# Where the load of x stands in SyncE's order: before or after the two transposes of a step

## The chip, the cores and the metric

The kernel runs on all 8 cores of one Trainium2 chip. Every core runs the same program on its own eighth of the tokens, and the cores do not talk to each other. The time is the device time of the slowest core in microseconds (us). Before the change it is 530.05 us, the median of three runs (528.37 to 530.62).

## What is computed

The input x is 2 x 16384 tokens of 1024 numbers. With xn the layer norm of x (no gain, no bias), the reference returns x + s * g:

```python
B = xn @ W2 + b2;  C = xn @ W3 + b3              # 16 columns each
delta = softplus(xn @ W1 + b1)                   # 1024 columns
h = xn[..., None] * einsum('bld,bln->bldn', delta, B)
s = einsum('bln,bldn->bld', C, h)                # = xn * delta * sum(B * C)
xh = xn @ H                                      # H: Hadamard matrix / 32
scale = max(abs(xh), axis=-1) / 7
xq = clip(round(xh / scale), -8, 7) * scale      # 4-bit activations
g = silu(xq @ tern(weight).T)                    # tern: -1, 0, +1 times a scale per row
```

## The kernel before

Each core has 4096 tokens, as 32 tiles of 128 tokens. A tile passes through a software pipeline. Each of the five engines has its own instruction stream with the same loop, `for c in range(-4, nt + 4)` with nt = 32, and in step c an engine works for several tiles, each at another stage. Semaphores alone tie the streams together. A waiting instruction holds up all that stands behind it on its engine. On ACT, DVE and POOL a helper (`Ser`, line 33) records every operation, so their line in the profile is always L33 and one goes by the names of the tiles.

What happens to tile t, with the step in which it happens:

- SyncE (SP in the profile) loads x into one of ten buffers, `xbuf[t % 10]` (**xb**), in step t-5 (line 176). From tile 10 on it waits first until the output tile that used the buffer is ready (semaphore sVOUT, line 175).
- ScalarE (ACT) squares and sums the tile in step t-4 (`dumpa<-xb`, called **the square** here; it is the first operation of an ACT step and waits for the load). VectorE (DVE) sums it in the same step (`xsm<-xb`). ACT makes the normalised bf16 tile `xnb` in step t-2.
- SyncE transposes xnb into **xnT** by a DMA in step t-2 (line 183), after a wait for xnb (line 179).
- GpSimd (POOL) makes sum and difference of the halves of xnT, uT and vT, in step t-1. TensorE (PE) multiplies xnT by W2 and W3 in step t-1 (line 303), by W1 (lines 268, 269) and, through uT and vT, by the Hadamard matrix (lines 312, 314) in step t.
- ACT makes delta in step t, and in step t+1 it rounds to 4 bits: `xqm`, then **xqb**.
- SyncE transposes xqb into **xqT** in step t+1 (line 191), after a wait for xqb (line 188).
- PE multiplies xqT by the ternary weight in step t+2 (lines 289, 290). In step t+3 DVE copies the product (`o3s`) and ACT makes the sigmoid from it with three operations (`esb<-psO`, `l`, `s`); they are the last of an ACT step.
- POOL and DVE combine in step t+4: t1b (POOL), t3b (DVE), t4b and ob (POOL), and POOL issues the store of the output tile (line 238).

So SyncE, whose stream holds nothing but DMAs and waits, goes in step c through three of them: the load of tile c+5, the transpose of xnb of tile c+2, the transpose of xqb of tile c-1. The load of tile c+5 is wanted by the square at the head of ACT's step c+1. The first five tiles are loaded ahead of the loop (line 169).

Of the kernel before, what the change touches and what calls it, by code (L numbers as in the profile page):

```python
# [62 lines left out]
def build_nc(nt=NT):  # L63
    tpc = nt * 128
    nc = bass.Bass("TRN2", target_bir_lowering=False)
    x_hbm = nc.dram_tensor("x", [tpc, DM], F32, kind="ExternalInput").ap()
# [14 lines left out]
    with ExitStack() as es:  # L81
# [22 lines left out]
        xbuf = [S(f"xb{i}", [128, DM], F32) for i in range(10)]  # L104
# [32 lines left out]
        sLDa = [SEM(f"sLD{i}") for i in range(10)]  # L137
# [22 lines left out]
        @block.sync  # L160
        def _(sp):
            sp.dma_start(out=c160s[:], in_=c160_hbm[:]).then_inc(sC160, 16)
            sp.dma_start(out=nc160s[:], in_=nc160_hbm[:]).then_inc(sC160, 16)
            sp.dma_start(out=identbf[:], in_=identbf_hbm[:]).then_inc(sWS, 16)
            sp.dma_start(out=identf[:], in_=identf_hbm[:]).then_inc(sWS, 16)
            sp.dma_start(out=onesbf[:], in_=onesbf_hbm[:]).then_inc(sWS, 16)
            sp.dma_start(out=onesf[:], in_=onesf_hbm[:]).then_inc(sWS, 16)
            for t in range(min(5, nt)):
                sp.dma_start(out=xbuf[t % 10][:], in_=x_hbm[t * 128:(t + 1) * 128, :]).then_inc(sLDa[t % 10], 16)
            sp.dma_start(out=Hs[:], in_=h_hbm[:]).then_inc(sWS, 16)  # L170
            for c in range(-4, nt + 4):
                t = c + 5
                if 5 <= t < nt:
                    if t >= 10:
                        sp.wait_ge(sVOUT, t - 9)
                    sp.dma_start(out=xbuf[t % 10][:], in_=x_hbm[t * 128:(t + 1) * 128, :]).then_inc(sLDa[t % 10], 16)
                t = c + 2
                if 0 <= t < nt:
                    sp.wait_ge(sXNB, t + 1)
                    if t >= 3:  # L180
                        sp.wait_ge(sPEBC, t - 1)
                        sp.wait_ge(sUVT, t - 2)
                    sp.dma_start(out=xnT[t % 3][:].rearrange("p (c n) -> p c n", c=KC),
                                 in_=xnbf[t % 8][:].rearrange("p (c n) -> p c n", c=KC),
                                 transpose=True).then_inc(sTXNa[t % 3], 16)
                t = c - 1
                if 0 <= t < nt:
                    sp.wait_ge(sXQB, t + 1)
                    if t >= 2:
                        sp.wait_ge(sPEO3, t - 1)  # L190
                    sp.dma_start(out=xqT[t % 2][:].rearrange("p (c n) -> p c n", c=KC),
                                 in_=xqbf[:].rearrange("p (c n) -> p c n", c=KC),
                                 transpose=True).then_inc(sTXQa[t % 2], 16)

        @block.gpsimd
        def _(g):
# [285 lines left out]
```

## Time and profile before

| | |
|---|---|
| median of three runs | 530.05 us (528.37 to 530.62) |
| the profiled execution | 529.42 us |
| span of its slowest core (core 3) | 527.9 us (all cores 525.0 to 527.9) |
| busy: PE, DVE, ACT, POOL | 66%, 58%, 65%, 61% of the span |
| mean granted TensorE clock | 0.881 on core 3 |

The span runs from the first to the last instruction of the core; the profiled execution's own time holds 1.5 us besides. The page cuts the span into 40 slices of 13.2 us and gives the busy share of each in tenths (9 is 90% or more):

```profile
PE   0014260997979697788788787787879798947100
DVE  1418886455766666766667667666675744442210
ACT  1613142569796979888888888888878878654220
POOL 6000160112677777777777777777777777767763
PEclk9998575799989899999899899989897989996755
DMA  7992321234656454554644455555656533222110
```

No engine is busy all the time. From slice 13 to slice 35 the pipeline is full and all rows are even; ahead of it the weights are prepared and the pipeline fills, behind it the pipeline drains. In a row of the timeline the numbers are start and duration in us, and in brackets stands how long the engine was idle before the instruction and who ended that. SPq and POOL rows of DMAs are the issue of the DMA; when its data have landed is told by a view of the DMA's line.

### The profile page before, as it was taken

Reading aid. Unit: us, or ns where it says so; the run is one execution under the profiler, and the core shown is the slowest. Engines: PE = TensorE matmul, PEld = TensorE weight load, DVE = VectorE, ACT = ScalarE, POOL = GpSimd, SP = SyncE. Lnnn points to the kernel's source line nnn. Section 1 sums busy time; section 2 is a strip of 40 time slices with the busy share of each in tenths; the row PEclk is TensorE's granted clock in tenths of the full one; section 3 lists DMA queues with packets and bytes.
Section 4 is the critical chain, followed back from the end, with each engine's and each line's share of the span. In section 5 each row is a group of like instructions: output and inputs, shape, how many; then the busy total and the mean of one; then the engine's idle time right before and its main releaser. Section 6 shows DMA issues by size and latency. Waiting matters only on the chain.

```text
span 527.9 us, 7193 instructions; the slowest of 8 cores (525.0 to 527.9 us)
## 1 busy us (share of the span) xinstructions
PE 349.0 (66%) x1696; PEld 149.0 (28%) x1696; DVE 304.7 (58%) x600; ACT 344.0 (65%) x393; POOL 323.0 (61%) x215
## 2 busy tenths in 40 slices
PE   0014260997979697788788787787879798947100
PEld 0001120443424243333333333333333343312000
DVE  1418886455766666766667667666675744442210
ACT  1613142569796979888888888888878878654220
POOL 6000160112677777777777777777777777767763
PEclk9998575799989899999899899989897989996755
DMA  7992321234656454554644455555656533222110
GB/s 136 247 261 81 103 61 23 57 89 79 134 111 128 120 122 119 120 122 119 120 120 121 120 120 120 121 121 128 128 128 136 137 84 95 66 61 60 43 77 40
DMA packets 80973, 57.78 MB, mean 109 GB/s; under 512 B 70435, under 2 KB 70564, under 8 KB 80932
## 3 DMA queue, kind: packets, MB, share of 16 engines
q1 hardware_dynamic: 72916, 34.19, 32.9%
q0 software_dynamic: 8016, 23.14, 13.5%
q8 instruction: 14, 0.23, 0.2%
q14 instruction: 27, 0.22, 0.1%
HBM read 25.93 MB, written 16.78 MB: 81 GB/s over the span
## 4 chain that ended last, share of the span: by engine, by line
POOL 48%; DVE 17%; issue 12%; PE 9%; DMA 5%; ACT 4%; POOLq 1%; DVEq 1%; SPq 1%; ACTq 0%
POOL ob L33 13%; POOL t4b L33 13%; POOL t1b L33 11%; DVE t3b L33 7%; POOL uT L33 5%; POOL vT L33 5%; DMA xnT<-xnb 3%; DVE tbf L33 3%; DMA xb<-x 2%; DVE absum L33 2%; PE psZ L268 2%; PE psZ L269 1%; PE psO L289 1%; PE psO L290 1%; DVE cst L33 1%
## 5 line engine op out<-in xcount | busy, mean ns | idle before, releaser
L33 POOL TENSOR_TENSOR t4b<-t3b,o3s 128x1024 f32<-128x1024 f32 x32 | 75.2, 2350 | 69.5 <-DVE t3b L33 69.5
L289 PE MATMUL psO<-ternT,xqT 128*128 128x512 bf16 x256 | 100.6, 393 | 19.3 <-DMA xqT<-xqb 14.1
L268 PE MATMUL psZ<-W1c,xnT 128*128 128x512 bf16 x256 | 101.0, 395 | 0.5 <-DVE bcw L33 0.5
L290 PE MATMUL psO<-ternT,xqT 128*128 128x512 bf16 x256 | 100.5, 393 | 0.0
L269 PE MATMUL psZ<-W1c,xnT 128*128 128x512 bf16 x256 | 100.1, 391 | 0.0
L312 PE MATMUL psXH<-Hs,uT 128*128 128x512 bf16 x128 | 57.1, 446 | 42.2 <-ACT xqm L33 40.0
L33 DVE SCALAR_TENSOR_TENSOR t3b<-xnb,cc,t1b 128x1024 f32<-128x1024 bf16 x32 | 41.1, 1285 | 66.7 <-POOL t1b L33 66.3
L33 POOL TENSOR_TENSOR ob<-xb,t4b 128x1024 f32<-128x1024 f32 x32 | 75.3, 2353 | 4.6
L33 POOL TENSOR_TENSOR t1b<-del,s 128x1024 f32<-128x1024 bf16 x32 | 68.5, 2141 | 7.9 <-ACT s L33 4.1
L33 ACT ACTIVATE esb<-psO,nsa 128x1024 f32<-128x1024 f32 x32 | 35.7, 1114 | 51.5 <-DVE o3s L33 51.0
L33 POOL TENSOR_TENSOR uT<-xnT 128x512 bf16<-128x512 bf16 x32 | 37.2, 1162 | 38.3 <-DMA xnT<-xnb 37.4
L314 PE MATMUL psXH<-Hs,vT 128*128 128x512 bf16 x128 | 57.3, 448 | 0.0
L33 ACT ACTIVATE esb<-psZ 128x1024 f32<-128x1024 f32 x32 | 32.8, 1024 | 31.0 <-PE psZ L271 28.9
L33 ACT ACTIVATE xqm<-psXH,c_s,inv 128x1024 bf16<-128x1024 f32 x32 | 38.5, 1205 | 18.0 <-DVE cc L33 15.4
L33 DVE COPY o3s<-psO 128x1024 f32<-128x1024 f32 x32 | 39.2, 1225 | 18.7 <-POOL ob L33 15.8
L33 DVE TENSOR_REDUCE xsm<-xb 128x1 f32<-128x1024 f32 x32 | 39.0, 1220 | 16.4 <-DMA xb<-x 13.4
L33 DVE TENSOR_REDUCE mx<-psXH 128x1 f32<-128x1024 f32 x32 | 39.2, 1224 | 9.1 <-PE psXH L314 6.1
L289 PEld LDWEIGHTS psO<-ternT,xqT 128*128 128x128 bf16 x256 | 25.7, 100 | 62.4 <-issue 37.6
L33 ACT ACTIVATE xnb<-xb,nmrs,rs 128x1024 bf16<-128x1024 f32 x32 | 39.7, 1241 | 3.2 <-ACT rs L33 0.3
L303 PE MATMUL psZ<-W23s,xnT 128*128 128x32 bf16 x256 | 11.4, 178 | 45.3 <-DMA xnT<-xnb 36.5
L33 POOL TENSOR_TENSOR vT<-xnT 128x512 bf16<-128x512 bf16 x32 | 36.9, 1152 | 4.6
L33 ACT ACTIVATE dumpa<-xb 128x1024 bf16<-128x1024 f32 x32 | 33.8, 1057 | 8.5 <-DMA xb<-x 6.0
(53 smaller groups left out, 510.8 us busy)
## 6 DMA issues: line engine op xcount, KB each, us to landing
xb<-x SPq DMA_DIRECT2D x32, 512.0 KB, 4.0
out<-ob POOLq DMA_DIRECT2D x32, 512.0 KB, 4.8
wfst<-wf POOLq DMA_DIRECT2D x8, 512.0 KB, 4.1
W1c<-w POOLq DMA_DIRECT2D x8, 256.0 KB, 18.3
Hs<-hpk SPq DMA_DIRECT2D x1, 512.0 KB
xnT<-xnb SPq DMA_TRANSPOSE x32, 6.1
xqT<-xqb SPq DMA_TRANSPOSE x32, 4.3
W23s<-w POOLq DMA_DIRECT2D x1, 64.0 KB, 3.4
```

The source lines that it names most:

```text
L33: inst = fn(*a, **kw)
L268: pe.matmul(psZ1[:, 0:512], lh, W1c[ic][:, 0:512], start=(ic == 0), stop=False)
L269: pe.matmul(psZ1[:, 512:1024], lh, W1c[ic][:, 512:1024], start=(ic == 0), stop=False)
L289: pe.matmul(ps[:, 0:512], lh, ternT[:, ic * DM:ic * DM + 512], start=(ic == 0), stop=(ic == KC - 1))
L290: last = pe.matmul(ps[:, 512:1024], lh, ternT[:, ic * DM + 512:(ic + 1) * DM], start=(ic == 0), stop=(ic == KC - 1))
L303: pe.matmul(psZ1[:, 0:32], xTn[:, ic * 128:(ic + 1) * 128], W23s[:, ic * 32:(ic + 1) * 32], start=(ic == 0), stop=False)
L312: pe.matmul(psXH[:, 0:512], uT2[t % 4][:, ic * 128:(ic + 1) * 128], Hs[:, ic * 512:(ic + 1) * 512], start=(ic == 0), stop=(ic == 3))
L314: last = pe.matmul(psXH[:, 512:1024], vT2[t % 4][:, ic * 128:(ic + 1) * 128], Hs[:, ic * 512:(ic + 1) * 512], start=(ic == 0), stop=(ic == 3))
```

## The change

The load of tile c+5 and its wait move from the head of SyncE's step to its end, behind the transposes of xnb and xqb. All else stays: the same DMAs, sizes, buffers and waits, and the same code on the other engines.

```diff
             for c in range(-4, nt + 4):
-                t = c + 5
-                if 5 <= t < nt:
-                    if t >= 10:
-                        sp.wait_ge(sVOUT, t - 9)
-                    sp.dma_start(out=xbuf[t % 10][:], in_=x_hbm[t * 128:(t + 1) * 128, :]).then_inc(sLDa[t % 10], 16)
                 t = c + 2
                 if 0 <= t < nt:
                     sp.wait_ge(sXNB, t + 1)
...
                     sp.dma_start(out=xqT[t % 2][:].rearrange("p (c n) -> p c n", c=KC),
                                  in_=xqbf[:].rearrange("p (c n) -> p c n", c=KC),
                                  transpose=True).then_inc(sTXQa[t % 2], 16)
+                t = c + 5
+                if 5 <= t < nt:
+                    if t >= 10:
+                        sp.wait_ge(sVOUT, t - 9)
+                    sp.dma_start(out=xbuf[t % 10][:], in_=x_hbm[t * 128:(t + 1) * 128, :]).then_inc(sLDa[t % 10], 16)
```

## Rows read from the trace of the kernel before

**Rows 1.** The page's chain of work that ended last, by engine.
```profile
POOL 48%; DVE 17%; issue 12%; PE 9%; DMA 5%; ACT 4%; POOLq 1%; DVEq 1%; SPq 1%; ACTq 0%
```

**Rows 2.** Timeline of POOL in the full pipeline, 299 to 320 us.
```profile
305.61 1.17 POOL L33 TENSOR_TENSOR uT<-xnT 128x512 bf16<-128x512 bf16 x1
...
312.29 2.36 POOL L33 TENSOR_TENSOR t4b<-t3b,o3s 128x1024 f32<-128x1024 f32 x1 [1.92 <-DVE t3b L33]
...
318.33 1.17 POOL L33 TENSOR_TENSOR uT<-xnT 128x512 bf16<-128x512 bf16 x1
```

**Rows 3.** Timeline of ACT, same stretch: one step, from square to square.
```profile
299.36 1.06 ACT L33 ACTIVATE dumpa<-xb 128x1024 bf16<-128x1024 f32 x1
...
301.19 1.24 ACT L33 ACTIVATE xnb<-xb,nmrs,rs 128x1024 bf16<-128x1024 f32 x1
...
306.08 1.15 ACT L33 ACTIVATE xqb<-xqm,nc_s 128x1024 bf16<-128x1024 bf16 x1
308.57 1.11 ACT L33 ACTIVATE esb<-psO,nsa 128x1024 f32<-128x1024 f32 x1 [1.34 <-DVE o3s L33]
...
312.08 1.06 ACT L33 ACTIVATE dumpa<-xb 128x1024 bf16<-128x1024 f32 x1
```

**Rows 4.** Timeline of SyncE's queue, same stretch: the three DMAs of one step.
```profile
304.51 0.33 SPq L176 DMA_DIRECT2D xb<-x  x1
305.04 1.22 SPq L183 DMA_TRANSPOSE xnT<-xnb  x1
307.36 2.58 SPq L191 DMA_TRANSPOSE xqT<-xqb  x1
```

**Rows 5.** Timeline of DVE, same stretch: its wait in a step.
```profile
310.62 1.28 DVE L33 SCALAR_TENSOR_TENSOR t3b<-xnb,cc,t1b 128x1024 f32<-128x1024 bf16 x1 [2.19 <-POOL t1b L33]
```

**Rows 6.** Timeline of SyncE's queue while the pipeline fills.
```profile
109.20 0.56 SPq L176 DMA_DIRECT2D xb<-x  x1
...
117.14 1.22 SPq L191 DMA_TRANSPOSE xqT<-xqb  x1
118.41 0.56 SPq L176 DMA_DIRECT2D xb<-x  x1
```

**Rows 7.** View of line 176, 89 to 122 us: three loads, each just behind xqT.
```profile
L176 SPq DMA_DIRECT2D xb<-x x3: 555/557/558, 90.8 to 118.4; - x3
...
DMA to landing us min/median/max: 4.9/5.0/5.3
```

**Rows 8.** View of line 176, all 27 loads of the loop.
```profile
DMA to landing us min/median/max: 3.6/4.0/5.9
```

**Rows 9.** View of line 191, 415 to 450 us: three transposes with no load near.
```profile
DMA to landing us min/median/max: 3.0/3.0/3.1
```

**Rows 10.** As rows 7, of core 2.
```profile
DMA to landing us min/median/max: 5.1/5.2/6.3
```

**Rows 11.** As rows 7, of core 6.
```profile
DMA to landing us min/median/max: 4.3/4.4/4.5
```

**Rows 12.** Timeline of ACT: the squares of steps 3, 4 and 27.
```profile
107.34 1.06 ACT L33 ACTIVATE dumpa<-xb 128x1024 bf16<-128x1024 f32 x1
...
122.35 1.06 ACT L33 ACTIVATE dumpa<-xb 128x1024 bf16<-128x1024 f32 x1
...
415.24 1.06 ACT L33 ACTIVATE dumpa<-xb 128x1024 bf16<-128x1024 f32 x1
```

**Rows 13.** Timeline of POOL: the t4b of steps 4 and 27.
```profile
131.24 2.35 POOL L33 TENSOR_TENSOR t4b<-t3b,o3s 128x1024 f32<-128x1024 f32 x1 [6.64 <-DVE t3b L33]
...
426.61 2.35 POOL L33 TENSOR_TENSOR t4b<-t3b,o3s 128x1024 f32<-128x1024 f32 x1 [1.92 <-DVE t3b L33]
```

**Rows 14.** Busy time by stretch: us, PE, PEld, DVE, ACT, POOL, granted clock, DMA share, GB/s.
```profile
263.00:314.00 51.00, 42.41 (x213) 18.19 (x213) 34.97 (x69) 41.94 (x50) 39.26 (x25) 0.97 0.50 124
...
466.00:528.00 62.00, 13.49 (x41) 4.72 (x40) 14.06 (x19) 17.61 (x16) 41.07 (x23) 0.65 0.18 59
```

**Rows 15.** View of waits: PE for xqT (us in total, times, longest).
```profile
PE psO L289 <- DMA xqT<-xqb: 14.1, 9, 4.6
```

## The prediction

> **What bounds the kernel now.** I read four views in this order: the chain of waits, the timeline of the engine that the chain names, the timelines of the engines that feed it, and the landing times of SyncE's DMAs.
>
> The chain lies on POOL for 48% of the span, far ahead of any other engine [rows 1]. In the timeline of the full pipeline POOL starts uT every 318.33 - 305.61 = 12.72 us [rows 2]. Within a step it is idle but for the 1.92 us in which DVE turns t1b into t3b, and DVE itself had waited 2.19 us for that t1b [rows 5]. So the pace of 12.7 us is POOL's own serial work. ACT keeps the same pace (square to square 312.08 - 299.36 = 12.72 us) with only one wait in it, 1.34 us for o3s [rows 3]. ACT thus needs about 11.4 us for a step. It is the engine with the least slack after POOL, and it is the engine that uses what SyncE loads.
>
> The reader should note two distances in ACT's step [rows 3]. From the square to the end of xqb it is 306.08 + 1.15 - 299.36 = 7.87 us, without a wait. From there to the next square it is 12.72 - 7.87 = 4.85 us, in which the three sigmoid operations and the 1.34 us of idleness lie.
>
> **The change part by part.** Nothing is added or removed. Three things move: the load, the wait for sVOUT ahead of it, and by that the issue times of both transposes.
>
> *The wait for sVOUT no longer stands ahead of xnT.* Before, SyncE sat until the output tile was ready and issued the load at 304.51 us and xnT at 305.04 [rows 4], although xnb had ended at 301.19 + 1.24 = 302.43 [rows 3]. Now xnT goes out about 2.6 us earlier. Who gains? POOL wants this xnT (tile c+2) only in its next step, at 318.33 in these rows [rows 2], 13.3 us after the old issue, and the chain of waits has PE for only 9% [rows 1]. I price it at 0; the cover is POOL's serial work, and it is worth nothing as long as POOL or ACT set the pace. With the cover gone it could be worth up to 2.6 us in some filling steps; it is not added.
>
> *xqT is issued with an emptier queue.* Its issue took 2.58 us with xnT 2.3 us ahead of it [rows 4] and 1.22 us where the queue was free [rows 6]. In the new order xnT is issued 4.8 us ahead of xqT, so I take 1.22 us. PE's waits for xqT are 14.1 us in total, in 9 pieces [rows 15], and they lie beside POOL's work. Price again 0.
>
> *The load is issued behind xqT.* This decides. SyncE's stream now holds the load of tile c+5 until xqb of step c has been made, and the square of that same tile is the first thing that ACT does in step c+1. That closes a loop which did not bind before: square, 7.87 us of ACT, xqb, SyncE, xqT, load, next square. Before, the load went out at 304.51, 7.6 us ahead of its square at 312.08, and landed about 4 us later. Now its length is:
> - ACT from the square to the end of xqb: 7.87 us [rows 3]
> - from there to the issue of xqT: 307.36 - 307.23 = 0.13 us [rows 3, 4]
> - from the issue of xqT to that of the load: 118.41 - 117.14 = 1.27 us [rows 6]
> - the load from issue to landing: not shown in this position in the full pipeline. Early on it is: while the pipeline filled, SyncE met no wait between xqT and the load of the next step, and three loads went out just behind an xqT, in the very order of the changed kernel. They took 4.9, 5.0 and 5.3 us [rows 7]. The median of all loads, most with no transpose ahead, is 4.0 us and the least 3.6 [rows 8]. Other cores have medians of 4.4 and 5.2 us in the same place [rows 10, 11]. A low bound is 4.0, a high bound 6.3 [rows 10]; I take 5.0, since these are rows of the same order and the slowest core is the one that counts
> - from landing to the square: 0.05 us, my estimate from the gaps of about 0.1 us between neighbours.
>
> The sum is 7.87 + 0.13 + 1.27 + 5.0 + 0.05 = 14.32 us a step, against 12.72. ACT's 1.34 us wait for o3s drops out, because the stall of about 3 us at the square absorbs it. Of the 6.45 us from xqb to landing, 4.85 were there before, so the net is 1.6 us a step.
>
> *Where it starts and ends.* The first squares see little of it: loads for steps 1 and 2 come within the preparation of the weights. The load for step 3 becomes the one issued at 109.20 [rows 6], behind the transposes of step 2; it lands at 109.20 + 5.0 = 114.2 us, where the square stood at 107.34 [rows 12]: 6.9 us late at once. From step 3 to the last square that needs a load, step 27, there are 24 periods: 114.2 + 24 x 14.32 = 457.9 us, against 415.24 [rows 12], so 42.7 us later. Then the drain follows. Part of the delay is given back, since POOL no longer trails ACT as far. The t4b of a step came 131.24 - 122.35 = 8.9 us after the square when POOL had just started, and 426.61 - 415.24 = 11.4 us after it at the end [rows 12, 13]. The return is between 0 and 2.5 us; I take 1.9, nearer to the first since POOL will have slack. Behind step 27 POOL has the same serial work as before. Sum: 42.7 - 1.9 = 40.8 us on a span of 527.9, that is 568.7; with the 1.5 us that the profiled execution (529.42) holds besides, 570.2 us. That execution lies 0.6 us below the median of the runs, which I leave out. Forecast: 570 us.
>
> *What else waits on SyncE.* Behind the load stands the wait for the next xnb, which needs an ACT step that itself waits for the load, so nothing is held up twice. The wait for sVOUT, moved behind xqT, is met: output tile c-5 is ready by the start of step c.
>
> *A rule to weigh.* The rows show 5.0 us for a load behind a transpose, against 4.0 for the others [rows 7, 8]. The Trainium skill, "DMA: Bandwidth & Descriptors", section "Anatomy of one DMA", says that some 2 us of a DMA are fixed and mostly completion latency, the rest bytes over bandwidth; for 512 KB that would be an estimate of 3.2 us. By that figure the loop would be 12.5 us, below POOL's pace, and the change would cost almost nothing. No load of this trace lands so soon, and the rule is stated for DMAs issued from POOL, so I hold to the rows. Ahead of each load the queue holds an xqT, which alone takes 3.0 us to land [rows 9]; 1.27 us of these are over when the load is issued.
>
> **The rivals.**
>
> *A: the load's latency passes beside xqT.* If the early loads were slow for another reason (all cores fetching at once), the load would land in 4.0 us in the full pipeline. For it: most loads do [rows 8]. Against it: in that early stretch all cores show more than 4.0, from 4.4 to 5.2 [rows 7, 10, 11]. The loop is then 13.32 us: 113.2 + 24 x 13.32 = 432.9, 17.7 us later, less 1.9, so 15.8 and 545 us. The values between belong to the forecast; I count as A what ends under 553.
>
> *B, on the other side: not slower.* The load lands within the 4.85 - 0.13 - 1.27 = 3.45 us that ACT leaves, and the earlier xnT and the shorter xqT pay. If all of PE's waits for xqT were on the path and went, 529 - 14 = 515 us; more likely a microsecond or two of the fill, 527. It decides at a landing of 3.45 us, and against it stands that the least of 27 is 3.6 [rows 8] and that the chain is POOL's.
>
> *C: PE becomes the bound.* In the full pipeline PE is busy for 42.41 of 51 us and is granted 0.97, next to the full 2.4 GHz; in the drain, busy for 13.49 of 62 us, it gets 0.65, a good part at 1.2 GHz [rows 14]. In the changed kernel PE has the same 10.6 us of work in 14.3 us, with idle gaps at the wait for ACT. At half the clock it would need up to 21 us a step; if a quarter of 24 steps went so, 6 x 7 = 42 us more, 612 us. Against it: its share falls only from 83% to 74%. The Trainium skill, "TensorE: Matmul & The Clock Gate", Part 1, has the clock fall after idle stretches; the low row of the drain agrees.
>
> *D: the load is later still.* Landings of 5.9 to 6.3 us as the norm, as the worst of these rows [rows 8, 10]: loop 15.3, 24 us more than the forecast, 594 us.
>
> **How the numbers follow.** Forecast (landing 4.4 to 5.6 us, 553 to 585 us) 75%; A 12%; B 3%; C 4%; D 6%. The range 547 to 584 us leaves out B, C, D and the low end of A, with some of the forecast's own tails. What a measurement can tell from no change is 0.5%, about 2.6 us. Faster by more 1%, within it 3%, slower 96%: B gives the first and part of the second.
>
> **What would show it.** In the full pipeline the square starts every 14.3 us, is idle about 3 us before and names the load as releaser; ACT's wait for o3s is gone; POOL gets idle time at t4b beyond 1.92 us. xqT's issue takes 1.22 us and the load's landing about 5.0. The square of step 27 stands near 458 us. The prediction is wrong if ACT's square still starts without a wait, if the period stays 12.7 us, or if the loop is 14.3 and the time still comes out elsewhere, which would mean that the drain or PE's clock was mis-sized.

## The result and the profile after

The changed kernel takes 555.54 us (median of ten runs, 553.25 to 559.86) against 530.24 us for the kernel before, measured beside it: ratio 1.0476, 95% interval 1.0446 to 1.0506. Forecast were 570 us and a range of 547 to 584. The direction and the mechanism were right, the size was 40 us where 25 came.

The slowest core of the profiled execution is core 6, with a span of 551.7 us. The chain of waits, by engine, answers to [rows 1]:

```profile
ACT 29%; DMA 22%; DVE 12%; POOL 12%; issue 12%; SPq 6%; PE 5%; ACTq 1%; DVEq 0%; POOLq 0%
```

POOL's share has gone from 48% to 12%. In its place stand ACT, the DMAs (19 of the 22% are the loads of x) and SyncE's queue: the three stations of the loop. The view of waits says the same (us in total, times, longest), first before the change, then after it:

```profile
POOL t4b L33 <- DVE t3b L33: 69.5, 32, 6.6
DVE t3b L33 <- POOL t1b L33: 66.3, 29, 8.8
...
ACT esb L33 <- DVE o3s L33: 51.0, 27, 6.7
...
ACT dumpa L33 <- DMA xb<-x: 6.0, 3, 3.8
```

```profile
POOL t4b L33 <- DVE t3b L33: 91.3, 32, 9.6
...
ACT dumpa L33 <- DMA xb<-x: 49.9, 28, 6.0
...
ACT esb L33 <- DVE o3s L33: 35.5, 22, 6.7
DVE t3b L33 <- POOL t1b L33: 35.5, 17, 8.8
```

28 squares wait for their load, where 3 did. DVE waits for POOL's t1b only 17 times where it had waited 29 times, and POOL waits longer for DVE (91.3 us for 69.5): POOL now follows. One step of the full pipeline, ACT first (answers to [rows 3]), then SyncE's queue (answers to [rows 4]):

```profile
304.55 1.06 ACT L33 ACTIVATE dumpa<-xb 128x1024 bf16<-128x1024 f32 x1 [2.42 <-DMA xb<-x]
...
311.48 1.15 ACT L33 ACTIVATE xqb<-xqm,nc_s 128x1024 bf16<-128x1024 bf16 x1
313.69 1.11 ACT L33 ACTIVATE esb<-psO,nsa 128x1024 f32<-128x1024 f32 x1 [1.07 <-DVE o3s L33]
...
317.99 1.06 ACT L33 ACTIVATE dumpa<-xb 128x1024 bf16<-128x1024 f32 x1 [0.88 <-DMA xb<-x]
```

```profile
308.00 1.40 SPq L178 DMA_TRANSPOSE xnT<-xnb  x1
312.75 1.23 SPq L186 DMA_TRANSPOSE xqT<-xqb  x1
314.09 0.52 SPq L193 DMA_DIRECT2D xb<-x  x1
```

xqb ends at 312.63. xqT follows 0.12 us later, the load 1.34 us after it, and the square starts at 317.99, which is 3.90 us after the load was issued. The period is 13.44 us. The load's line, first the three of 88 to 125 us, then the 17 of 200 to 430 us (answer to [rows 7, 8]):

```profile
L193 SPq DMA_DIRECT2D xb<-x x3: 570/570/570, 90.7 to 122.1; - x3
...
DMA to landing us min/median/max: 4.1/4.5/4.6
...
L193 SPq DMA_DIRECT2D xb<-x x17: 522/522/534, 205.8 to 422.0; - x17
...
DMA to landing us min/median/max: 3.6/3.9/4.5
```

The squares of steps 3, 4 and 27 and the t4b of step 27 answer to [rows 12, 13]:

```profile
112.75 1.06 ACT L33 ACTIVATE dumpa<-xb 128x1024 bf16<-128x1024 f32 x1 [6.00 <-DMA xb<-x]
...
126.27 1.06 ACT L33 ACTIVATE dumpa<-xb 128x1024 bf16<-128x1024 f32 x1 [2.13 <-DMA xb<-x]
...
439.68 1.06 ACT L33 ACTIVATE dumpa<-xb 128x1024 bf16<-128x1024 f32 x1 [2.21 <-DMA xb<-x]
```

```profile
450.42 2.35 POOL L33 TENSOR_TENSOR t4b<-t3b,o3s 128x1024 f32<-128x1024 f32 x1 [3.98 <-DVE t3b L33]
```

With these the whole difference is accounted for. The square of step 27 is 439.68 - 415.24 = 24.4 us late. The t4b of that step comes 10.74 us behind it where it was 11.37, so 0.6 us come back. From that t4b to the end it is 101.3 us in both kernels. 24.4 - 0.6 = 23.8, and the spans differ by 551.7 - 527.9 = 23.8. (The profiled execution, 553.25 us, is the shortest of the ten; their median lies 2.3 us above it.)

### The profile page after: what moved, and what is told of

It is laid out like the page before. It is cut to its first block, busy times and chain, and to the rows that moved or that the text cites. A ratio compares the mean times of both kernels' runs of the same rounds, so it can differ in the third digit from the quotient of the medians.

```text
span 551.7 us, 7193 instructions; the slowest of 8 cores (543.4 to 551.7 us)
## 1 busy us (share of the span) xinstructions
PE 364.1 (66%) x1696; PEld 152.2 (28%) x1696; DVE 320.6 (58%) x600; ACT 344.3 (62%) x393; POOL 323.2 (59%) x215
## 4 chain that ended last, share of the span: by engine, by line
ACT 29%; DMA 22%; DVE 12%; POOL 12%; issue 12%; SPq 6%; PE 5%; ACTq 1%; DVEq 0%; POOLq 0%
DMA xb<-x 19%; ACT xqm L33 5%; ACT xnb L33 5%; SPq L186 5%; ACT xqb L33 5%; ACT esb L33 5%; ACT del L33 5%; POOL t4b L33 4%; POOL ob L33 4%; POOL t1b L33 3%; DMA xnT<-xnb 3%; DVE tbf L33 3%; DVE t3b L33 2%; DVE absum L33 2%; DVE cst L33 1%
## 5 line engine op out<-in xcount | busy, mean ns | idle before, releaser
L33 POOL TENSOR_TENSOR t4b<-t3b,o3s 128x1024 f32<-128x1024 f32 x32 | 75.3, 2353 | 91.3 <-DVE t3b L33 91.3
L268 PE MATMUL psZ<-W1c,xnT 128*128 128x512 bf16 x256 | 105.0, 410 | 0.5 <-DVE bcw L33 0.5
L269 PE MATMUL psZ<-W1c,xnT 128*128 128x512 bf16 x256 | 103.0, 402 | 0.0
L312 PE MATMUL psXH<-Hs,uT 128*128 128x512 bf16 x128 | 63.2, 494 | 50.4 <-ACT xqm L33 48.3
L33 ACT ACTIVATE dumpa<-xb 128x1024 bf16<-128x1024 f32 x32 | 33.9, 1058 | 50.2 <-DMA xb<-x 49.9
L314 PE MATMUL psXH<-Hs,vT 128*128 128x512 bf16 x128 | 63.6, 497 | 0.0
L33 DVE SCALAR_TENSOR_TENSOR t3b<-xnb,cc,t1b 128x1024 f32<-128x1024 bf16 x32 | 41.1, 1284 | 37.2 <-POOL t1b L33 35.5
L33 ACT ACTIVATE esb<-psO,nsa 128x1024 f32<-128x1024 f32 x32 | 35.7, 1115 | 36.5 <-DVE o3s L33 35.5
L33 ACT ACTIVATE esb<-psZ 128x1024 f32<-128x1024 f32 x32 | 32.8, 1024 | 26.9 <-PE psZ L271 24.4
L33 ACT ACTIVATE xqm<-psXH,c_s,inv 128x1024 bf16<-128x1024 f32 x32 | 38.5, 1204 | 16.8 <-DVE cc L33 14.1
L33 DVE TENSOR_SCALAR bcw<-psZ 128x32 f32<-128x32 f32 x32 | 6.1, 192 | 65.9 <-PE psZ L305 65.6
```

The costliest lines, as they stand in the source:

```text
L33: inst = fn(*a, **kw)
L268: pe.matmul(psZ1[:, 0:512], lh, W1c[ic][:, 0:512], start=(ic == 0), stop=False)
L269: pe.matmul(psZ1[:, 512:1024], lh, W1c[ic][:, 512:1024], start=(ic == 0), stop=False)
L312: pe.matmul(psXH[:, 0:512], uT2[t % 4][:, ic * 128:(ic + 1) * 128], Hs[:, ic * 512:(ic + 1) * 512], start=(ic == 0), stop=(ic == 3))
L314: last = pe.matmul(psXH[:, 512:1024], vT2[t % 4][:, ic * 128:(ic + 1) * 128], Hs[:, ic * 512:(ic + 1) * 512], start=(ic == 0), stop=(ic == 3))
```

## The experiments

The theory L: the loss is the loop from the square over xqb, SyncE, xqT and the load to the next square. The rivals: T, the new order of the DMAs' traffic itself; P, PE's granted clock, which fell from 0.88 to 0.84 in the mean of the span. A landing is the time from the issue of a DMA until its data are there. Each of the first six kernels keeps some of the change and breaks or keeps the loop. Ratios are to the kernel before, measured in the same session, with 95% intervals.

**The load between the two transposes** (as the changed kernel, but the five lines of the load stand ahead of the wait for xqb).

```diff
                 # xnT
+                (load of tile c + 5)
                 # wait for xqb, xqT
-                (load of tile c + 5)
```

> The load stands between the two transposes: behind xnT, but ahead of the wait for xqb. Theory L (the loss is the loop square, xqb, xqT, load, next square): the load goes out when the output tile is ready, about 5 us after the square as before the change, so no square waits in the full pipeline, the period is 12.7 us, and the time is 528 to 532 us. Rival T (the loss is the new order of traffic, xnT issued early and meeting other DMAs): xnT is as early as in the changed kernel, so most of the loss stays, 545 to 556 us. Rival P (PE's granted clock, 0.84 instead of 0.88): as T if the early xnT causes it.

Measured: 528.68 us, ratio 0.9966 (0.9943 to 0.9990). SyncE's queue in the full pipeline:

```profile
301.66 1.22 SPq L178 DMA_TRANSPOSE xnT<-xnb  x1
303.31 0.33 SPq L185 DMA_DIRECT2D xb<-x  x1
306.42 1.25 SPq L191 DMA_TRANSPOSE xqT<-xqb  x1
```

xnT goes out ahead of the load, as in the changed kernel, and nothing is lost. What costs must lie behind the wait for xqb. With that T falls as far as it blames the early xnT. The gain of 0.3% is at the edge of what can be told. The loads themselves land later in this place. This is the view of line 185 on the same core (core 3), 200 to 430 us:

```profile
DMA to landing us min/median/max: 5.0/5.2/7.5
```

Before the change the median was 3.9 us there. It costs nothing here, because the load goes out long enough ahead of its square.

**The load behind the wait for xqb, but ahead of xqT.**

```diff
                     sp.wait_ge(sXQB, t + 1)
                     if t >= 2:
                         sp.wait_ge(sPEO3, t - 1)
+                    (load of tile c + 5)
                     sp.dma_start(out=xqT[t % 2]..., transpose=True)
-                (load of tile c + 5)
```

(The load takes its wait for sVOUT along. The load of tile 5, whose step has no xqT, is issued at the end of step 0.)

> As the changed kernel, but the load is issued after the wait for xqb and ahead of the transpose into xqT. Theory L: the loop loses the 1.33 us of xqT's issue and is 7.88 + 0.13 + 4.0 + 0.14 = 12.2 us, under POOL's 12.7, so POOL sets the pace again in the full pipeline; about 1 to 3 us are left from the filling steps: 531 to 533 us. If being queued behind a transpose makes the load slower, its landing falls under the changed kernel's median of 4.1 us; if not, it stays 3.9 to 4.1. Rivals T and P: the traffic is nearly that of the changed kernel, 548 to 556 us.

Measured: 530.55 us, ratio 1.0009 (0.9987 to 1.0030). Two squares in the full pipeline, and the landing of its loads from 200 to 430 us (core 0):

```profile
312.76 1.06 ACT L33 ACTIVATE dumpa<-xb 128x1024 bf16<-128x1024 f32 x1
...
325.46 1.06 ACT L33 ACTIVATE dumpa<-xb 128x1024 bf16<-128x1024 f32 x1
```

```profile
DMA to landing us min/median/max: 3.7/4.1/5.0
```

Period 12.70 us, no wait for the load. So the wait for xqb alone is harmless; the 1.3 us of xqT's issue behind it carry the loop from 12.2 us over POOL's 12.7. And a load with xqT behind it lands no sooner (core means 4.0 to 4.3 us) than one with xqT ahead of it in the changed kernel (3.6 to 4.0 us): being queued behind xqT costs nothing that can be seen here. Right behind xnT loads took longer, as the run before showed; the last section comes back to that.

**SyncE's order of the changed kernel, with eleven buffers and the load one tile further ahead.**

```diff
-        xbuf = [S(f"xb{i}", [128, DM], F32) for i in range(10)]
+        xbuf = [S(f"xb{i}", [128, DM], F32) for i in range(11)]
...
-                t = c + 5
+                t = c + 6
                 if 5 <= t < nt:
-                    if t >= 10:
-                        sp.wait_ge(sVOUT, t - 9)
+                    if t >= 11:
+                        sp.wait_ge(sVOUT, t - 10)
```

(Buffers and their semaphores are taken modulo 11 throughout.)

> The changed kernel's order of SyncE, but with eleven buffers for x and the load one tile further ahead (tile c+6 in step c). Theory L: the load lands a whole step before its square, the square never waits, and the period is 12.7 us: 527 to 531 us. Rivals T and P: order and traffic are as in the changed kernel, 548 to 556 us.

Measured: 529.79 us, ratio 0.9995 (0.9966 to 1.0025). Only 2 squares still wait for a load, 3.8 us in all. The order of the three DMAs is not the cause. What costs is that the load is issued too shortly ahead of its square.

**The square behind xnb**, SyncE as in the changed kernel.

```diff
-                (square of tile c + 4)
                 (lnv, rs of tile c + 3)
                 (xnb of tile c + 2)
+                (square of tile c + 4)
```

> SyncE exactly as in the changed kernel; on ACT the square moves behind xnb within the step. Theory L: from the square to the end of xqb it is 7.88 - 1.92 = 5.96 us, the loop is 5.96 + 0.13 + 1.33 + 4.05 + 0.14 = 11.6 us and no longer binds, the period is POOL's 12.7 us: 528 to 533 us. Rivals T and P: nothing changes in the DMAs' order, 550 to 556 us.

Measured: 532.37 us, ratio 1.0040 (1.0014 to 1.0065). One step of ACT:

```profile
304.37 1.06 ACT L33 ACTIVATE dumpa<-xb 128x1024 bf16<-128x1024 f32 x1 [0.64 <-DMA xb<-x]
...
309.23 1.15 ACT L33 ACTIVATE xqb<-xqm,nc_s 128x1024 bf16<-128x1024 bf16 x1
...
317.82 1.06 ACT L33 ACTIVATE dumpa<-xb 128x1024 bf16<-128x1024 f32 x1
```

From the square to the end of xqb it is 6.0 us (309.23 + 1.15 - 304.37), and 23 of the 25 us are gone with every DMA in the changed order. T is refuted by this run. P is not decided by it: the mean clock is back at 0.862 to 0.880 together with the time, and no run held the clock fixed. Against P stands the loop itself. None of its stations is work of PE, ACT goes from the square to the end of xqb in 7.88 us in nearly every step of the full pipeline of either kernel, and what ACT waits for PE's work in this stretch did not grow: 28.9 us in all for psZ before the change and 24.4 us after it, and 15.4 and 14.1 us for cc, which DVE makes from PE's psXH.

**The two halves of the change.** Loads from tile 10 on at the end of the step, then only the loads of tiles 5 to 9.

```diff
+                if 5 <= t < nt and t < 10:     # at the head   (other run: t >= 10)
...
+                if 5 <= t < nt and t >= 10:    # at the end    (other run: t < 10)
```

> Loads of tiles 5 to 9 at the head of SyncE's step as before the change, those of tiles 10 to 31 at its end as in the changed kernel. Theory L: no late start; from the square of step 6 to that of step 27 there are 21 periods of about 13.5 instead of an average of 12.75 us, 15 to 16 us, of which about 2 come back in the drain: 542 to 546 us. A rival in which the loss arises while the pipeline fills expects 530 to 534.

> The other half: only the loads of tiles 5 to 9 move to the end of SyncE's step. Theory L: the squares of steps 3 to 5 come some 5 to 7 us late as in the changed kernel, POOL's first t4b about 5 us late, and POOL, which sets the pace from there on, does not make it up: 533 to 536 us. Together with the run from tile 10 on the losses add to that of the changed kernel, 25 us, within 4 us. The rival of the fill expects 550 or more.

Measured: 549.02 us, ratio 1.0358 (1.0318 to 1.0398), and 537.07 us, ratio 1.0128 (1.0101 to 1.0155). Both are above what was expected, by 3 and 1 us. The losses against 529.88 us are 19.1 and 7.2 us, in sum 26.3 against 25.3 for the whole change. So the late start of steps 3 to 5 is a quarter of the loss, the longer period three quarters. The first run also explains its own miss, since its cores differ: a period of about 13.5 us was expected, and the slowest core has 13.77. Here the period is (square of step 27 - square of step 6) / 21, and the landing the mean of the last 17 loads:

```text
core                 0      1      2      3      4      5      6      7
mean landing, us   3.72   3.94   3.70   3.87   3.72   3.88   4.21   4.17
period, us        13.40  13.63  13.34  13.48  13.32  13.50  13.77  13.72
span, us          540.5  546.8  537.8  543.1  535.5  541.7  549.4  548.8
```

From core to core the period grows by about 0.8 us for each us of landing, and the time is that of the core with the slowest loads.

**Half the load** from tile 10 on (the other 512 columns keep what an older tile left there).

```diff
-                    sp.dma_start(out=xbuf[t % 10][:], in_=x_hbm[t * 128:(t + 1) * 128, :])...
+                    w = DM if t < 10 else DM // 2
+                    sp.dma_start(out=xbuf[t % 10][:, 0:w], in_=x_hbm[t * 128:(t + 1) * 128, 0:w])...
```

> The changed kernel, but from tile 10 on only the first 512 of the 1024 columns of x are loaded (the rest of the buffer keeps an older tile, so half of x is left out). Theory L: the landing falls from about 3.9 to about 3.2 us, and the period of every step whose square waits is 9.48 us + landing: 12.7 us or less, where POOL's pace takes over; 5 us are left from the filling steps: 533 to 537 us. A rival in which the load's place in the order costs something of itself, whatever its length, expects 550.

Measured: 549.07 us, ratio 1.0331 (1.0168 to 1.0493, from two executions). The time was missed. The 22 half loads of its slowest core (core 4):

```profile
DMA to landing us min/median/max: 2.8/3.7/4.6
```

That core is not typical. From 200 to 430 us the core means of the landing are 3.0 to 3.6 us, 3.3 in the mean of all eight, against 3.6 to 4.0 and 3.9 in the changed kernel: half the bytes took off 0.5 us, where 0.7 was expected. A step whose square waits keeps to the formula: 355.54 - 341.95 = 13.59 us, and its load landed in 4.12 us (9.48 + 4.12 = 13.60). On core 0, whose half loads land in 3.0 us in the mean, the steps that wait go down to 12.2 us, as L says. But every few steps one has no wait for the load and about 3 us of waiting for o3s:

```profile
345.53 1.11 ACT L33 ACTIVATE esb<-psO,nsa 128x1024 f32<-128x1024 f32 x1 [3.08 <-DVE o3s L33]
...
349.04 1.06 ACT L33 ACTIVATE dumpa<-xb 128x1024 bf16<-128x1024 f32 x1
```

The square before this one stands at 334.08, so this step took 15.0 us, and the mean period of the core is 13.04 us and not 12.7. L is borne out for the steps in which the load is waited for. Its expectation that POOL's pace of 12.7 us takes over smoothly was wrong, and why the mean stays above 12.7 is open.

**t1b ahead of uT and vT on POOL**, once in the changed kernel and once in the kernel before.

```diff
             for c in range(-4, nt + 4):
+                (t1b of tile c - 4)
                 (uT, vT of tile c + 1)
-                (t1b of tile c - 4)
                 (wait for t3b, t4b, ob, store of tile c - 4)
```

> The changed kernel, and on POOL t1b goes ahead of uT and vT, so that DVE's t3b runs beside these two and POOL's wait of 1.92 us goes: POOL then needs about 10.8 us a step. Theory L: POOL's gain is worth nothing here, since the loop of the load sets 13.4 to 13.6 us: 545 to 555 us, like the changed kernel. A rival in which POOL's own work still sets the pace of the changed kernel expects about 1.9 us less for some 25 steps, 505 to 515 us.

> The same exchange on POOL in the kernel before. Theory L: POOL's 10.8 us fall under ACT's 11.4, which then sets the pace: period 11.5 to 12 us instead of 12.7 for some 24 steps, 505 to 518 us; the fill and the drain stay as they are. If instead something else sets 12.7 us (PE, DVE), the time stays at 527 to 531.

Measured: 554.63 us, ratio 1.0460 (1.0411 to 1.0509), in the changed kernel; 520.17 us, ratio 0.9820 (0.9791 to 0.9849), in the kernel before. The same edit is worth 10 us where POOL sets the pace and nothing where the load does. In the changed kernel DVE's t3b can now run beside uT and vT, and yet POOL waits for it as long as without the exchange (91.3 us, see above):

```profile
POOL t4b L33 <- DVE t3b L33: 90.2, 32, 6.8
```

In the kernel before the gain fell short of the expected 12 to 25 us: the period is 12.25 us, and ACT has a wait in each step:

```profile
304.71 1.11 ACT L33 ACTIVATE esb<-psO,nsa 128x1024 f32<-128x1024 f32 x1 [0.93 <-DVE o3s L33]
```

**Towards a faster kernel.** The exchange on POOL with the load in the middle, and the exchange on POOL with SyncE as before, while DVE copies o3s ahead of bcw, prod and dot.

```diff
+                (o3s of tile c - 3)
                 (bcw, prod, dot of tile c + 1)
-                (o3s of tile c - 3)
                 (t3b of tile c - 4)
```

> The exchange on POOL (t1b ahead of uT and vT) together with the load between the two transposes of SyncE's step. Theory L: the square of a tile never waits in either order, so the place of the load in front of the wait for xqb is worth nothing more: 518 to 521 us, as with the exchange alone (520.2). If the earlier xnT mattered once POOL is faster, 2 us or more would come off, 516 to 518.

> The exchange on POOL with SyncE as before the change, and on DVE the copy o3s goes ahead of the three operations on B and C (bcw, prod, dot), which wait for PE. With the exchange alone ACT waits 0.9 us a step for o3s, and the period is 12.25 us. If that wait is what keeps ACT from its own 11.4 us, the period falls to 11.4 to 11.6 us, 24 steps by 0.7 to 0.8 us, and the time to 500 to 506 us. If PE or DVE itself binds, it stays at 515 to 521.

Measured: 521.46 us, ratio 0.9818 (0.9786 to 0.9850), so the place of the load is worth nothing further as long as it stands ahead of xqb, although its loads land in 6.1 to 6.9 us (core means) here; and 504.10 us, ratio 0.9521 (0.9480 to 0.9562), the fastest kernel of this study. ACT in the latter:

```profile
294.73 1.06 ACT L33 ACTIVATE dumpa<-xb 128x1024 bf16<-128x1024 f32 x1
...
301.46 1.15 ACT L33 ACTIVATE xqb<-xqm,nc_s 128x1024 bf16<-128x1024 bf16 x1
302.70 1.11 ACT L33 ACTIVATE esb<-psO,nsa 128x1024 f32<-128x1024 f32 x1
```

The wait for o3s is gone in this step, and ACT runs without a break. Over the whole span ACT still waits 24.4 us for o3s, in 14 pieces. Many steps take 11.47 us from square to square, which is ACT's own work; the mean of steps 6 to 27 is 11.7 us.

## Why the prediction was right, and where it was off

The mechanism was right: the loop binds, and it starts and ends where the prediction said. That the time fell inside the range is partly luck. Put the measured landing of 4.06 us in place of 5.0 into the prediction's own sum, and it gives a loop of 13.38 us and a time of 546.6 us, just under the range. The smaller terms of the loop, a smaller return in the drain and the 2.3 us between the profiled execution and the median brought it back to 555.5.

- *POOL's work of 12.7 us set the pace before*: right. The exchange on POOL gains 1.8% in the kernel before and nothing in the changed one.
- *The wait for sVOUT ahead of xnT, and xqT's emptier queue, priced at 0*: right. With both in place and the load ahead of xqb the time is 528.68 us, 0.3% under the kernel before. xqT's issue took 1.23 us as said.
- *The loop*: right in its stations, off in one length. On average of the 24 periods from step 3 to step 27 of core 6: square to end of xqb 7.90 us (forecast 7.87), to xqT 0.13 (0.13), to the load 1.37 (1.27), landing 4.06 (5.0), landing to square 0.15 (0.05); in sum 13.62.
- *The landing of the load is the term that was mis-sized.* It was forecast 0.9 us too long; the small terms give back 0.2. The loop was 13.62 instead of 14.32 us, over 24 steps 16.8 of the 18.2 us by which the square of step 27 was forecast too late (457.9, it came at 439.68). I had taken 5.0 from three loads behind an xqT and read the order into it. The order alone does not make them slow: with xqT ahead but in the changed kernel, core 3's three took 4.1, 4.3 and 4.4 us and core 6's 4.1, 4.5 and 4.6, and in the full pipeline a place behind xqT shows no cost. The mean of these three over all cores goes from 3.9 us (the run with the load ahead of xqT) to 4.9 (before), and with xqT ahead from 4.1 to 4.9. So a part of xqT in that stretch is not ruled out. What sets the landing there stays open; all eight cores fetch nearly together, but no run varied that. The prediction also read too much into its cores. Core 4's three have a median of 4.3 us, below the 4.4 that it gives as the least, and cores 0 and 1 have medians of 4.4 and 4.5 us in the full pipeline too (180 to 410 us), with no transpose just ahead.
- *The late start*: forecast 114.2 us for the square of step 3; it stood at 112.75. The load was issued at 108.11 and not at 109.20, which is 1.1 us of it, and it landed in 4.5 us and not in 5.0.
- *The return in the drain*: 1.9 us forecast, 0.6 came.
- *ACT's wait for o3s* was to be gone. It fell from 51.0 to 35.5 us in all and stands in 22 steps. It lies inside the same pause of ACT, so the squares wait less for their load than the 3 us forecast (49.9 us in 28 pieces), and the length of the loop stays the same.
- *Rival A* (4.0 us, 545 us) had the landing right. It came out 10 us low: the landing was 0.06 us longer and the smaller terms 0.23 us longer a step, the return was 1.3 us smaller, and the median lies 2.3 us above the profiled execution. The measured landing is A's and not the 4.4 to 5.6 us of the forecast's own case, though the time lies in that case's range. A deserved more than the 12% that I gave it: 17 loads of the full pipeline stood against three of the fill.
- *The rule of the Trainium skill* ("DMA: Bandwidth & Descriptors", "Anatomy of one DMA", by my estimate 3.2 us for 512 KB): no full load landed so soon in the profile of the changed kernel (least 3.4 us on any core), and the measurement decides. Its part for the bytes agrees better: halving 512 KB would save an estimated 0.6 us by it, and the half load saved 0.5 us in the mean of the cores.
- *Rival C*: the granted clock did fall, from 0.97 to 0.89 in the stretch 263 to 314 us (answer to [rows 14]), and in the drain from 0.65 to 0.59. No cost of it shows: the loop does not pass through PE, and from the t4b of step 27 to the end it is 101.3 us in both kernels. The stretch 263 to 314 us after the change:

```profile
263.00:314.00 51.00, 38.16 (x184) 15.89 (x182) 33.22 (x62) 38.94 (x46) 36.25 (x23) 0.89 0.41 109
```

- *Rivals B and D* did not come. Landings of 6 us and more are possible in the full pipeline, as the exchange with the load in the middle shows, but not in this order.

## What to carry to other kernels

A prefetch is as early as its place in the queue's order lets it be: a DMA that waits for nothing itself still waits for all that its queue waits for. Before such a transfer is moved, follow the loop that it closes (consumer, what the consumer releases, the queue, the transfer, the consumer again), add its stations from the timeline and compare the sum with the present period; the cost is the difference times the number of steps, plus the late start once. For a latency that the loop turns on, take the value from the stretch in which the loop will run and from all cores, and not from a few early instances that happen to have the right order.

## What was not expected of the hardware

A load of 512 KB has no fixed landing. It differs with the kernel and with the core, and whether a transpose stands ahead of it in the queue does not settle it. These are the least and the greatest of the eight core means, loads issued from 200 to 430 us, one execution of each kernel:

```text
kernel                                     mean landing, us
before (xnT and the store right behind)    3.9 to 4.5
changed (xqT 1.3 us ahead)                 3.6 to 4.0
load ahead of xqT                          4.0 to 4.3
eleven buffers (xqT 1.3 us ahead)          3.7 to 4.9
square later (xqT 1.3 us ahead)            3.7 to 4.8
load right behind xnT                      4.2 to 5.5
the same, with the exchange on POOL        6.1 to 6.9
```

In the last two rows xnT is issued just ahead of the load, and the store of the output tile, a DMA of POOL, within 1.5 us of it on either side. Which of the two costs the time was not tested. Nor is it known why cores differ by over 1 us in the rows with the same order.

And operations of VectorE and GpSimd that run at the same time can hold one another up. In the kernel before, t3b takes 1.28 us and no operation of POOL runs beside it. In the fastest kernel it takes 1.95 us where it begins 0.9 us before the end of POOL's uT, and vT, which begins 0.94 us before the end of that t3b, takes 1.95 us instead of 1.15. In each pair the one that began second is longer by 0.7 to 0.8 us, nearly the time that both run, and uT, the first, keeps its usual time:

```profile
292.37 1.95 DVE L33 SCALAR_TENSOR_TENSOR t3b<-xnb,cc,t1b 128x1024 f32<-128x1024 bf16 x1
```

```profile
283.77 2.35 POOL L33 TENSOR_TENSOR t4b<-t3b,o3s 128x1024 f32<-128x1024 f32 x1 [1.47 <-DVE t3b L33]
...
292.09 1.16 POOL L33 TENSOR_TENSOR uT<-xnT 128x512 bf16<-128x512 bf16 x1
293.38 1.95 POOL L33 TENSOR_TENSOR vT<-xnT 128x512 bf16<-128x512 bf16 x1
295.48 2.35 POOL L33 TENSOR_TENSOR t4b<-t3b,o3s 128x1024 f32<-128x1024 f32 x1
```

So POOL takes 295.48 - 283.77 = 11.71 us for this step without a wait for another engine, and not the 10.8 that I had reckoned. With the 11.47 us of ACT's own work that fits a mean period of 11.7 us; no run took the overlap away to show it.
